# Residual tokens built by GpSimd in SBUF from the turned normed tokens, instead of being turned by TensorE and passed through DRAM

## The chip, the cores and the metric

The kernel runs on one core of one Trainium2 chip. The metric is device time in microseconds (us). The kernel before was timed three times: 315.67, 315.70 and 314.47 us, median 315.67 us. TensorE is PE in the profile, VectorE DVE, ScalarE ACT, GpSimd POOL, and SP is the engine that issues nearly all DMAs.

## The reference, cut to what matters

Input x is (4, 128, 32, 32): four images ("batches" here) of 128 channels and 1024 positions. Three layers follow each other, and each image passes them alone.

```
x = x + nin(softmax(q k^T) v)            # group norm, full attention over 1024 positions, one head
t = to_tokens(x)                         # (4, 1024, 128)
t = t + linear_attention(ln(t))          # softmax over keys, 4 heads
n = ln(t)                                # (t - mean) / sqrt(var + 1e-5), per token
logits = n @ router_w.T ; probs = softmax(logits) ; rw, re = top_k(probs, 2) ; rw = rw / rw.sum()
out = n
for e in range(8):
    out = out + combine[:, e:e+1] * (gelu(n @ w1[e] + b1[e]) @ w2[e] + b2[e])
t = t + out                              # so the result is t + n + the experts' sum
```

The change is about the term t + n of the last line, called the residual tokens. With spread s = sqrt(var + 1e-5) it is also n (1 + s) + mean.

## The kernel before, in words

Matrix products are made of fp32r parts: each operand is split into a high and a low part and three products are summed. An image's 1024 positions are 8 tiles of 128, or 2 halves of 512.

The program has two phases. In the first, each pass of a loop over images b runs the attention of image b, the linear attention's keys of image b-1 (la), and the end of the linear attention and the routing of image b-2 (lc). The first image has an opening of its own, the second a pass written out, and b = 2 and b = 3 are the passes of a hardware loop. In the second phase the experts of all four images run: 16 steps per image (2 halves by 8 experts), 64 steps in all, numbered through. The remaining linear attention and routing of images 2 and 3 are put between these steps, by tables that say at which step: TAIL_AT and END_AT (L67 and L68) for TensorE, ScalarE and VectorE, POOL_AT (L73) for the order on GpSimd. GpSimd doesn't step with the others: it takes its functions in that order, each held only by its own waits.

A step on the engines: TensorE makes the hidden product into one of two PSUM banks (L1468 to L1470), ScalarE applies Gelu (L871), VectorE multiplies by the token's share of the expert (L1354, both inputs in SBUF), ScalarE and VectorE split the product into high and low (L882, L1363), and TensorE makes the outward product five steps later. Some steps (WHOLE) use one product in full fp32 instead of three (L1831). Each engine runs its own program in order. PSUM banks are handed round: a unit (u0, lT, z0, ...) is a use of a bank, TensorE fills it after the earlier unit in the bank was drained.

What the change touches:

- second_norm (L595) makes the normed tokens w_n of t2 on GpSimd, token by partition, by layer_norm (L574): two small operations and a power (L581 to L585) for each half, then 8 of 128x128 (L590). TensorE turns w_n to channel by partition (turn_w), and its high and low parts stay in wT_hi and wT_lo.
- normed_residual (L598) adds w_n to t2 in 8 operations (L601). TensorE turns the sum in 8 transposes (turn_z, units z0 and z1), ScalarE drains them (L783) into out_s in the loop and xb later, SP stores 512 KB to DRAM (L400), and load_routed (L416) brings it back half by half into z_in (L422). result (L1366) adds it to the experts' sum in PSUM.
- first_norm (L604) makes the normed tokens u of the linear attention. In the second phase GpSimd has second_norm(2), first_norm(3), normed_residual(2), add_bout(3), second_norm(3), normed_residual(3), in this order. TensorE turns the halves of u at steps 15 and 17.
- The routing (route, L1176) is a chain of some 22 small VectorE operations from the turned logits (L1187) to the shares in comb (L1224). TensorE turns comb in two units c0 and c1, VectorE copies them (L1167), SP stores them (L407, L408). After the loop SP issues load_routed(0, 0) and load_routed(0, 1), and then the first shares (L463), broadcast to all partitions. The first multiply of the experts (L1354) waits for these. Image 3's first shares go the same way after step 42 (L441).
- b2_parts and cb_in: one product (L1827) adds the experts' output biases, weighted by the shares, with 16 rows of high and 16 of low parts.

## Time and profile before

| what | us |
|---|---|
| median of three runs | 315.67 |
| the profiled execution, its own time | 317.83 |
| its span, first to last instruction | 316.0 |
| PE busy | 301.5 (95%) |
| DVE busy | 256.2 (81%) |
| ACT busy | 200.4 (63%) |
| POOL busy | 156.9 (50%) |

The profile is of one execution. Its own time is 2.16 us above the median of the three. PE's busy time counts matmuls whose ends are modelled, so what counts below is the distance from one start to the next, and an idle gap that names who ended it. The first phase ends near 186 us.

### The profile page before, as it was taken

To read this page: it belongs to the slowest core of one execution; us is meant where nothing else is said; L and a number is where in the kernel's file an instruction comes from. 1 tells how busy PE (TensorE), PEld (TensorE's weight loads), DVE (VectorE), ACT (ScalarE), POOL (GpSimd) and SP (SyncE) were. 2 spreads that over 40 slices of the span, in tenths; PEclk is the share of its full clock that TensorE was granted. 3 is DMA by queue.
4 is the path that set the end of the run, shared out by engine and by line. 5 is a ranking of instruction groups with operands and counts; after the bars stand their busy time and mean duration, and the time that the engine had idled before them with its cause. 6 is when DMAs were issued, how large, how long until landed. Compare 5 with 4: busy or idle time off the path is not lost.

```text
span 316.0 us, 5527 instructions
## 1 busy us (share of the span) xinstructions
PE 301.5 (95%) x1592; PEld 239.3 (76%) x1592; DVE 256.2 (81%) x641; ACT 200.4 (63%) x352; POOL 156.9 (50%) x357
## 2 busy tenths in 40 slices
PE   7998989989999999999999998999999999998996
PEld 5787768866878887878888796887776876666885
DVE  5598698587587798987698986999998897796996
ACT  3468473656771587664279576559777556785992
POOL 3898890149941985970684400399932069100000
PEclk9599999999999999999999999999999999999999
DMA  5902000020000021000000118295602881227911
GB/s 129 337 14 66 2 0 2 0 68 0 1 3 0 2 66 44 26 12 0 0 1 0 66 25 242 115 419 221 208 8 97 311 317 40 73 81 299 350 34 66
DMA packets 12904, 29.61 MB, mean 94 GB/s; under 512 B 2208, under 2 KB 6224, under 8 KB 10960
## 3 DMA queue, kind: packets, MB, share of 16 engines
q1 hardware_dynamic: 12448, 28.87, 26.4%
q10 hardware_dynamic: 432, 0.46, 0.4%
q8 instruction: 10, 0.16, 0.2%
q14 instruction: 14, 0.11, 0.1%
HBM read 24.73 MB, written 4.59 MB: 93 GB/s over the span
## 4 chain that ended last, share of the span: by engine, by line
PE 71%; DVE 14%; DMA 6%; issue 4%; ACT 3%; SPq 1%; DVEq 0%; ACTq 0%
PE ring L1483 10%; PE ring L1468 8%; PE ring L1470 8%; PE ring L1469 8%; PE scores L1468 7%; PE scores L1470 7%; PE scores L1469 7%; PE ring L1831 3%; DMA k_both<-scratch_s 3%; DVE pT_lo L1071 3%; DVE prob L1064 2%; PE ring L1648 2%; PE ring L1626 2%; PE ring L1613 2%; DMA scratch_c<-xT 1%
## 5 line engine op out<-in xcount | busy, mean ns | idle before, releaser
L871 ACT ACTIVATE gel<-scores,b_c 128x512 f32<-128x512 f32 x64 | 43.8, 685 | 18.7 <-PE scores L1470 15.0
L1071 DVE TENSOR_TENSOR pT_lo<-ring,pT_hi 128x512 fp32r<-128x512 f32 x64 | 40.5, 681 | 9.7 <-ACT pT_hi L730 9.5
L724 ACT ACTIVATE prob<-prob,row_max 128x1024 f32<-128x1024 f32 x32 | 36.8, 1150 | 11.5 <-DVE prob L1064 11.5
L581 POOL TENSOR_SCALAR rstd<-lmv 128x4 f32<-128x4 f32 x16 | 4.5, 283 | 76.1 <-DVE lmv L1106 74.8
L1064 DVE TENSOR_SCALAR_CACHE_REDUCE prob<-scores 128x1024 f32<-128x1024 f32 x32 | 38.7, 1216 | 3.4 <-PE scores L1470 2.9
L730 ACT ACTIVATE pT_hi<-ring 128x512 fp32r<-128x512 f32 x64 | 34.6, 599 | 9.2 <-PE ring L1483 8.9
L1483 PE MATMUL ring<-ident,prob 128*128 128x128 f32 x256 | 33.9, 275 | 3.4 <-DVE pT_lo L1071 2.1
L1483 PEld LDWEIGHTS ring<-ident,prob 128*128 128x128 f32 x256 | 28.7, 140 | 8.4 <-DVE pT_lo L1071 2.7
L1468 PE MATMUL scores<-wT_hi,w_hi 128*128 128x512 f32 x64 | 30.1, 470 | 1.7 <-ACT gel L871 1.7
L1468 PE MATMUL scores<-k_both,q_hi 128*128 128x512 f32 x64 | 27.0, 422 | 0.7 <-DVE prob L1064 0.7
L1468 PE MATMUL ring<-pT_hi,v_hi 128*128 128x512 f32 x64 | 26.6, 416 | 0.8 <-DVE pT_lo L1071 0.8
L1470 PE MATMUL scores<-k_both,q_lo 128*128 128x512 f32 x64 | 25.1, 393 | 0.0
L1470 PE MATMUL scores<-wT_hi,w_lo 128*128 128x512 f32 x64 | 25.1, 392 | 0.0
L1469 PE MATMUL scores<-wT_lo,w_hi 128*128 128x512 f32 x64 | 25.1, 392 | 0.0
L1469 PE MATMUL scores<-k_both,q_hi 128*128 128x512 f32 x64 | 25.1, 391 | 0.0
L1470 PE MATMUL ring<-pT_hi,v_lo 128*128 128x512 f32 x64 | 25.0, 391 | 0.0
L1469 PE MATMUL ring<-pT_lo,v_hi 128*128 128x512 f32 x64 | 25.0, 390 | 0.0
L734 ACT ACTIVATE o_s<-ring 128x512 f32<-128x512 f32 x8 | 4.8, 598 | 27.4 <-PE ring L1470 27.4
L590 POOL TENSOR_SCALAR u<-t,rstd 128x128 f32<-128x128 f32 x32 | 20.4, 654 | 0.9 <-POOL rstd L585 0.9
L612 POOL TENSOR_TENSOR t<-t,bout_row 128x128 f32<-128x128 f32 x32 | 14.0, 476 | 12.6 <-PE ring L1483 7.5
L590 POOL TENSOR_SCALAR w_n<-t,rstd 128x128 f32<-128x128 f32 x32 | 17.2, 551 | 0.9 <-POOL rstd L585 0.9
L1468 PEld LDWEIGHTS scores<-wT_hi,w_hi 128*128 128x128 f32 x64 | 12.1, 189 | 6.7 <-ACT gel L871 4.1
(304 smaller groups left out, 794.5 us busy)
## 6 DMA issues: line engine op xcount, KB each, us to landing
pT_hi<-scratch_s SPq DMA_DIRECT2D x8, 1024.0 KB, 7.4
prob<-scratch_s SPq DMA_DIRECT2D x4, 1024.0 KB, 7.6
k_both<-scratch_s SPq DMA_DIRECT2D x3, 1024.0 KB, 5.9
z_in<-scratch_z SPq DMA_DIRECT2D x8, 256.0 KB, 3.2
out_dram<-out_s SPq DMA_DIRECT2D x7, 256.0 KB, 2.4
xb<-in_x_dram SPq DMA_DIRECT2D x3, 512.0 KB, 3.2
scratch_z<-out_s SPq DMA_DIRECT2D x2, 512.0 KB, 2.8
k_both<-scratch_s SPq DMA_DIRECT2D x4, 256.0 KB, 5.5
```

What stands on the lines that cost most here:

```text
L590: last = pool.tensor_scalar(dst[:, j, :], src[:, j, :], neg[:, j:j + 1], std[:, j:j + 1], ALU.add, ALU.mult)
L612: last = pool.tensor_tensor(tiles_piece(t2, n), tiles_piece(t1, n), tiles_piece(bout_b, n), ALU.add)
L724: act.activation(prob[:, i % 2, :], prob[:, i % 2, :], ACT.Exp, bias=row_max[:, i:i + 1], scale=-1.0, accum_out=row_sum[:, 0, i:i + 1]).th ...
L730: act.activation(tile_group(pT_hi, n, i), as_tiles(ps(place, unit)), ACT.Copy).then_inc(p_hi_made, 1)
L871: act.activation(half(gel, s % 2), scores[:, s % 2, :], ACT.Gelu, bias=b1_c[:, s % E:s % E + 1]).then_inc(e_gelu, 1)
L1064: dve.tensor_scalar(prob[:, i % 2, :], scores[:, 2 * (i % 2):2 * (i % 2) + 2, :].rearrange("p a t -> p (a t)"), -SCALE, None, ALU.mult, AL ...
L1071: dve.tensor_tensor(tile_group(pT_lo, n, i), as_tiles(ps(place, unit)), tile_group(pT_hi, n, i).bitcast(FP32), ALU.subtract).then_inc(drai ...
L1468: pe.matmul(dst, lh, rh, start=start, stop=False)
L1469: pe.matmul(dst, lh, rl, start=False, stop=False)
L1470: return pe.matmul(dst, ll, rh, start=False, stop=stop)
L1483: last = pe.transpose(dst[0:t.shape[-1], j * step:j * step + rows], t, ident[0:rows, 0:rows])
L1831: last = pe.matmul(dst, tile(w2_s, e), hs_ring[step % RING], start=e == 0, stop=e == closing(m, h))
```

## The change: what it does

- normed_residual, TensorE's turn_z, ScalarE's turn_z, the store (L400), the load (L422) and their semaphores go, for all four images.
- second_norm gets five small operations on 128x8 after its normed tokens, which put the spreads 1 + s and the high and low parts of the means into free columns of comb, and a wait at its end of the norm for the earlier store of comb's copy. They ride on the transpose c0 and on the store of the shares, which has 88 rows in place of 64.
- load_spreads broadcasts the 1 + s of each half to all partitions: 256 KB a half into SBUF. load_routed loads no residual, but two rows of means a half. These rows meet two rows of ones in b2_parts, so the product of the biases adds the means too.
- add_parts (8 operations of 128x128) adds wT_hi and wT_lo into z_of[m], and residual_of (8 more) multiplies by the spreads, both on GpSimd. Image 0's two and image 1's add_parts run before second_norm(2); image 1's residual_of after first_norm(3); image 2's after add_bout(3); image 3's after second_norm(3).
- The wait of add_bout for unit z1 goes. kT1 takes bank 0 in place of 2 in the loop. Image shares are staged in hw in place of z_in.

```diff
-ROUTING = dict(o=["o0", "o1"], w=["w0", "w1"], lg=["lg0", "lg1"], z=["z0", "z1"], c=["c0", "c1"])
+ROUTING = dict(o=["o0", "o1"], w=["w0", "w1"], lg=["lg0", "lg1"], c=["c0", "c1"])
...
-                  T3a=0, T3b=1, lg0=2, lg1=3, u0=0, u1=1, lT=2, z0=3, z1=0, kT0=1, kT1=2, PV0=3, T4a=0,
+                  T3a=0, T3b=1, lg0=2, lg1=3, u0=0, u1=1, lT=2, kT0=1, kT1=0, PV0=3, T4a=0,
...
-              + ROUTING["z"] + LINEAR["p"] + ROUTING["c"] + ["g"])
+              + LINEAR["p"] + ROUTING["c"] + ["g"])
...
-POOL_AT = dict(n2=2, n1=5, nr=12, ab=21, n2e=32, nre=38)
+POOL_AT = dict(n2=2, n1=5, z=12, ab=21, n2e=32, ze=44)
+SPREADS, MEANS = 2 * E, 2 * E + HALVES
+SHARE_ROWS = (2 * E + 3 * HALVES) * QUAD
+MEAN_ROW = 64
...
-    scratch_s = nc.dram_tensor("scratch_s", (B, HALVES * E * QUAD, P), FP32).ap()
+    scratch_s = nc.dram_tensor("scratch_s", (B, SHARE_ROWS, P), FP32).ap()
...
+        minus_one = sb("minus_one", [P, TILES])
+        means = sb("means", [P, TILES])
...
-        zT_early, cT_early = out_s[:, :], (z_in[0:TILES * E, 0:P], z_in[:, P:2 * P])
-        zT_late = xb[:, :]
-        cT_late = (xT[0:TILES * E, 0, :], xT[:, 1, :])
+        cT_early = (hw[0:SHARE_ROWS, 0:P], hw[:, P:2 * P])
+        cT_late = (xT[0:SHARE_ROWS, 0, :], xT[:, 1, :])
+        z_of = [z_in, xb, z_in, xb]
+        spread_of = [out_s[:, :]] + [m[:, :].bitcast(FP32) for m in (v_hi, v_lo, v_hi)]
...
-            def store_residual(place, lc, zT):
-                for unit in ROUTING["z"]:
-                    wait_drained(sp, place, unit)
-                    apart(sp)
-                sp.dma_start(scratch_z[bass.ds(lc * HALVES, HALVES)].rearrange("h c t -> c h t"),
-                             zT.rearrange("c (h t) -> c h t", h=HALVES)).then_inc(z_stored, 16)
...
-            def load_routed(m, h):
-                sp.wait_ge(z_stored, 16 * (m + 2))
-                apart(sp)
+            def shares_of(m, e0, ne):
+                rows = scratch_s[m, e0 * QUAD:(e0 + ne) * QUAD, :].rearrange("r t -> (r t)")
+                return rows.rearrange("(a t) -> a t", a=1).to_broadcast([P, ne * BANK])
+            def load_spreads(m):
                 sp.wait_ge(c_stored, 32 * (m + 2))
                 apart(sp)
-                sp.dma_start(half(z_in, h), scratch_z[m * HALVES + h]).then_inc(z_loaded[h], 16)
+                for h in range(HALVES):
+                    if m == B - 1:
+                        sp.wait_ge(z_ready[h], B - 2)
+                        apart(sp)
+                    sp.dma_start(half(spread_of[m], h), shares_of(m, SPREADS + h, 1)).then_inc(spread_loaded[h], 16)
+            def load_routed(m, h):
+                sp.wait_ge(c_stored, 32 * (m + 2))
+                apart(sp)
+                for n in range(2):
+                    row = MEANS + n * HALVES + h
+                    sp.dma_start(cb_in[MEAN_ROW + n:MEAN_ROW + n + 1, h, :].bitcast(FP32),
+                                 scratch_s[m, row * QUAD:(row + 1) * QUAD, :].rearrange("(a j) t -> a (j t)", a=1)
+                                 ).then_inc(c_loaded[h], 16)
                 parts = 2 * E * QUAD
                 for r in (0, QUAD * E):
...
-            sp.sem_inc(z_stored, 16)
             sp.sem_inc(c_stored, 32)
             load_x(1)
             load_x(2)
             with sp.Fori(2, B - 1) as b:
                 load_x(b + 1)
-                store_residual(loop_place(b), b - 2, zT_early)
                 store_shares(loop_place(b), b - 2, cT_early)
-            store_residual(loop_place(B - 1), B - 3, zT_early)
+            load_spreads(0)
             store_shares(loop_place(B - 1), B - 3, cT_early)
...
+            load_spreads(1)
...
-            sp.wait_ge(xb_read, B)
-            store_residual(TAIL, B - 2, zT_late)
             store_shares(TAIL, B - 2, cT_late)
+            load_spreads(2)
...
-            store_residual(END, B - 1, zT_late)
             store_shares(END, B - 1, cT_late)
             load_shares(3, 0)
+            load_spreads(3)
...
                 layer_norm(1, lc, t2, w_n, w_made)
-            def normed_residual(lc):
-                pool.wait_ge(w_made, lc * HALVES + HALVES)
-                for n in range(PIECES):
-                    last = pool.tensor_tensor(tiles_piece(t2, n), tiles_piece(t2, n), tiles_piece(w_n, n), ALU.add)
-                last.then_inc(z_made, 1)
+                pool.wait_ge(c_stored, lc * 32 + 32)
+                apart(pool)
+                at = 2 * E * QUAD
+                spread, high, low = (comb[:, 0, at + n * TILES:at + (n + 1) * TILES] for n in range(3))
+                std, neg = (rstd[1][:, i, :] for i in range(2))
+                pool.tensor_tensor(spread, std, minus_one[:, :], ALU.pow).then_inc(spread_chain, 1)
+                pool.tensor_scalar(means[:, :], neg, -1.0, 0.0, ALU.mult, ALU.add)
+                pool.tensor_scalar(high.bitcast(FP32R), neg, -1.0, 0.0, ALU.mult, ALU.add).then_inc(spread_chain, 1)
+                pool.wait_ge(spread_chain, lc * 2 + 2)
+                apart(pool)
+                pool.tensor_scalar(spread, spread, 1.0, 1.0, ALU.mult, ALU.add)
+                pool.tensor_tensor(low, means[:, :], high, ALU.subtract).then_inc(spread_made, 1)
+            def add_parts(place, m):
+                wait_drained(pool, place, "w1")
+                if m == 1:
+                    pool.wait_ge(xb_read, B)
+                for h in range(HALVES):
+                    if m > 1:
+                        wait_drained(pool, y_place(m - 2), f"y{h}")
+                    w_hi, w_lo = (half(w[:, m * T:(m + 1) * T], h).bitcast(FP32) for w in (wT_hi, wT_lo))
+                    dst = half(z_of[m], h)
+                    for n in range(QUAD):
+                        last = pool.tensor_tensor(tile(dst, n), tile(w_hi, n), tile(w_lo, n), ALU.add)
+                    last.then_inc(z_added, 1)
+            def residual_of(m):
+                for h in range(HALVES):
+                    pool.wait_ge(z_added, m * HALVES + h + 1)
+                    pool.wait_ge(spread_loaded[h], m * 16 + 16)
+                    dst, spread = half(z_of[m], h), half(spread_of[m], h)
+                    for n in range(QUAD):
+                        last = pool.tensor_tensor(tile(dst, n), tile(dst, n), tile(spread, n), ALU.mult)
+                    last.then_inc(z_ready[h], 1)
             def first_norm(lb):
                 layer_norm(0, lb, t1, u, u_made)
-            def add_bout(lb, routed):
-                if routed is not None:
-                    wait_filled(pool, routed, "z1")
+            def add_bout(lb):
...
-            pool.memset(b2_parts[:, :].bitcast(FP32), 0.0)
+            after(pool.memset(b2_parts[:, :].bitcast(FP32), 0.0))
+            after(pool.memset(b2_parts[MEAN_ROW:MEAN_ROW + 2, :].bitcast(FP32), 1.0))
...
-                    normed_residual(lc)
                 first_norm(la)
-                add_bout(la, place if lc is not None else None)
+                add_bout(la)
             batch(SECOND, 1, 0, None)
             pool.wait_ge(gn_made, 3)
             with pool.Fori(2, B) as b:
                 batch(loop_place(b), b, b - 1, b - 2)
             norms = gathered(
+                (0, lambda: add_parts(loop_place(2), 0)),
+                (0, lambda: residual_of(0)),
+                (0, lambda: add_parts(loop_place(B - 1), 1)),
                 (POOL_AT["n2"], lambda: second_norm(B - 2)),
                 (POOL_AT["n1"], lambda: first_norm(B - 1)),
-                (POOL_AT["nr"], lambda: normed_residual(B - 2)),
-                (POOL_AT["ab"], lambda: add_bout(B - 1, TAIL)),
+                (POOL_AT["z"], lambda: residual_of(1)),
+                (POOL_AT["ab"], lambda: add_bout(B - 1)),
+                (POOL_AT["ab"], lambda: add_parts(TAIL, 2)),
+                (POOL_AT["ab"], lambda: residual_of(2)),
                 (POOL_AT["n2e"], lambda: second_norm(B - 1)),
-                (POOL_AT["nre"], lambda: normed_residual(B - 1)),
+                (POOL_AT["ze"], lambda: add_parts(END, B - 1)),
+                (POOL_AT["ze"], lambda: residual_of(B - 1)),
...
-            def turn_z(place, lc, zT):
-                act.wait_ge(z_stored, lc * 16 + 16)
-                for n in range(HALVES):
-                    unit = f"z{n}"
-                    wait_filled(act, place, unit)
-                    act.activation(half(zT, n), ps(place, unit), ACT.Copy).then_inc(drained[place.bank(unit)], 1)
...
-                dve.wait_ge(z_loaded[h], m * 16 + 16)
+                dve.wait_ge(z_ready[h], m + 1)
                 if not first_batch(m):
                     dve.wait_ge(stored[h], m * 16)
-                dve.tensor_tensor(half(out_s, h), ps(place, f"y{h}"), half(z_in, h), ALU.add
+                dve.tensor_tensor(half(out_s, h), ps(place, f"y{h}"), half(z_of[m], h), ALU.add
...
-            def turn_z(place, lb):
-                pe.wait_ge(z_made, lb + 1)
-                for n in range(HALVES):
-                    turn(place, f"z{n}", tiles_of(t2, n))
             def turn_comb(place, lb):
                 pe.wait_ge(c_made, lb + 1)
+                pe.wait_ge(spread_made, lb + 1)
...
-                    pe.wait_ge(c_loaded[h], m * 32 + 32)
+                    pe.wait_ge(c_loaded[h], m * 64 + 64)
```

## Rows read from the trace of the kernel before

**Rows 1.** Busy time by stage: us, then each engine's busy us (instructions), clock, DMA share, GB/s.
```profile
91.50:141.70 50.20, 49.24 (x293) 39.93 (x293) 42.22 (x118) 30.53 (x58) 32.56 (x78) 1.00 0.07 24
141.70:191.00 49.30, 48.97 (x298) 40.73 (x299) 41.27 (x118) 30.22 (x58) 19.10 (x44) 1.00 0.07 21
215.00:240.00 25.00, 24.97 (x122) 18.87 (x122) 23.15 (x50) 20.50 (x36) 18.91 (x25) 1.00 0.36 126
265.00:292.00 27.00, 24.77 (x106) 17.13 (x104) 21.58 (x51) 19.29 (x32) 4.43 (x8) 1.00 0.35 130
```

**Rows 2.** The chain of waits in order of time: start, us, what.
```profile
185.99 1.79 DMA scratch_c<-z_in
...
190.79 4.67 DMA k_both<-scratch_s
...
234.28 0.87 PE scores L1483 x8
...
281.29 3.83 DMA scratch_c<-xT
285.26 4.75 DMA k_both<-scratch_s
```

**Rows 3.** VectorE's timeline, routing in pass b = 2: start, us, instruction.
```profile
122.43 0.29 DVE L1187 TENSOR_REDUCE logit<-ring 128x64 f32<-128x128 f32 x1 [0.21 <-PE ring L1671]
...
129.17 0.40 DVE L1203 TENSOR_TENSOR rt<-rt,falling 128x64 f32<-128x64 f32 x1
...
133.04 2.47 DVE L1071 TENSOR_TENSOR pT_lo<-ring,pT_hi 128x512 fp32r<-128x512 f32 x4
```

**Rows 4.** VectorE's timeline, the same instructions in pass b = 3.
```profile
172.57 0.29 DVE L1187 TENSOR_REDUCE logit<-ring 128x64 f32<-128x128 f32 x1 [0.21 <-PE ring L1671]
...
178.71 0.22 DVE L1203 TENSOR_TENSOR rt<-rt,falling 128x64 f32<-128x64 f32 x1
...
181.93 2.48 DVE L1071 TENSOR_TENSOR pT_lo<-ring,pT_hi 128x512 fp32r<-128x512 f32 x4
```

**Rows 5.** GpSimd's timeline in both passes.
```profile
127.32 3.52 POOL L556 TENSOR_SCALAR h_f<-xb,affine 128x128 f32<-128x128 f32 x8 [0.21 <-POOL affine L542]
...
173.65 3.36 POOL L612 TENSOR_TENSOR t<-t,bout_row 128x128 f32<-128x128 f32 x8 [3.77 <-PE ring L1483]
```

**Rows 6.** SP's timeline: the stores of the shares in both passes, the loads after them.
```profile
136.33 0.52 SPq L407 DMA_DIRECT2D scratch_s<-z_in  x1
...
185.49 0.45 SPq L407 DMA_DIRECT2D scratch_s<-z_in  x1
...
187.96 0.32 SPq L422 DMA_DIRECT2D z_in<-scratch_z  x1
```

**Rows 7.** GpSimd's timeline in the second phase.
```profile
201.78 0.43 POOL L581 TENSOR_SCALAR rstd<-lmv 128x4 f32<-128x4 f32 x1 [24.77 <-DVE lmv L1106]
...
211.55 0.19 POOL L581 TENSOR_SCALAR rstd<-lmv 128x4 f32<-128x4 f32 x1
...
215.93 10.02 POOL L590 TENSOR_SCALAR u<-t,rstd 128x128 f32<-128x128 f32 x8 [0.22 <-POOL rstd L585]
```

**Rows 8.** GpSimd's powers on gsum: us summary by form, ns min/median/max.
```profile
L537 POOL TENSOR_TENSOR gsum<-gsum,minus_half x3: 563/564/708, 7.5 to 57.3; 128x1 f32<-128x1 f32 x2, 128x2 f32<-128x2 f32 x1
```

**Rows 9.** TensorE's timeline: u turned at steps 15 and 17.
```profile
221.79 0.60 PE L1483 MATMUL ring<-ident,u 128*128 128x128 f32 x4
...
226.00 0.66 PE L1483 MATMUL scores<-ident,u 128*128 128x128 f32 x4
```

**Rows 10.** Around image 3's first shares: ScalarE's and TensorE's timelines.
```profile
279.07 0.58 ACT L783 ACTIVATE xb<-scores 128x512 f32<-128x512 f32 x1
...
292.12 0.50 PE L1468 MATMUL scores<-wT_hi,w_hi 128*128 128x512 f32 x1 [1.34 <-ACT gel L871]
```

**Rows 11.** VectorE's multiplies (L1354) by stretch: us, busy (count), clock, DMA.
```profile
224.00:230.00 6.00, 2.44 (x3) 1.00 0.60 210
...
292.00:311.00 19.00, 9.63 (x15) 1.00 0.52 178
```

29 lines of the change are left out of this document (11 added, 18 removed).

## The prediction

> **What bounds the kernel now.** I read the busy time by stage first. In the second phase TensorE is the bound: 24.97 us of the 25 from 215 to 240 are PE's, and DVE has only 1.85 us free there [rows 1]. In the two loop passes PE is busy 98 and 99%, DVE 84%. Then the chain of waits in order of time: it runs through PE except in three places that this change touches. After the loop it goes from the store of the shares to the first share load, 4.67 us to landing at 190.79, and around 281 to 290 it does the same for image 3, 3.83 us for the store and 4.75 us for the load [rows 2]. In pass b = 2 it goes through VectorE's routing, of which the timelines show more [rows 3, 4]. Last I read the timelines of POOL and PE for what POOL makes just in time [rows 7, 9].
>
> The reader should see that removed PE work is worth its time only where PE is what the chain goes through, and that POOL, although half idle, feeds PE at one point with no slack.
>
> **PE loses the turned residuals.** Eight transposes cost PE 0.87 us (234.28) [rows 2], so 3.5 us for four images.
>
> Pass b = 2 gives nothing of it. The routing starts from the turned logits, which PE makes before the residual, at 122.43, and ends when the pT_lo of tile 4 can start at 133.04, 10.61 us later [rows 3]. PE needs these drains before it goes on to the turned keys and comb. If PE comes 0.87 us earlier, it waits 0.87 us longer: 0.
>
> In pass b = 3 the same stretch took 9.36 us, 172.57 to 181.93 [rows 4], and there PE and DVE arrive nearly together. The difference of 1.25 us has a cause in the trace: in b = 2 POOL works beside the routing (group norm from 127.32 on), in b = 3 it ends at 173.65 + 3.36 = 177.0 and the operations after that are short (the multiply by falling 0.22 us against 0.40) [rows 3 to 5]. The change fills this hole. POOL does add_bout(2) up to 3.8 us earlier, as its wait for z1 goes, and then add_parts(0), residual_of(0) and add_parts(1): 24 operations at 3.36 / 8 = 0.42 us, 10.1 us [rows 5], or from about 173.3 to 183.4. So the routing of b = 3 becomes as slow as that of b = 2. The part behind 177.0 holds most of the difference; I take +0.85 us, bounds 0 and +1.25, and PE's 0.87 us are again not seen.
>
> Here the Trainium skill ("SBUF — State Buffer", Who interferes with whom) has a rule: a VectorE instruction with two SBUF inputs contends with a GpSimd instruction that reads SBUF, and one with a single SBUF input does not. By that rule the trace agrees: the pT_lo drains, with one input in PSUM, keep 0.62 us each in both passes, and the routing operations stretch. The rule also says that the loser waits for the whole instruction, which would make the cost in the expert phase much larger than the measured means give; that is a rival below.
>
> **The way to the first share.** SP issues the store of the shares 13.90 us after the turned logits in b = 2 (136.33 against 122.43) and 12.92 us after in b = 3 (185.49 against 172.57) [rows 3, 4, 6]. With a routing like that of b = 2, it comes +0.98 us later. Then SP issues load_routed for both halves: six DMAs from 187.96 until the first share load at 190.79, 0.47 us each [rows 2, 6]. The two residual loads go and four of means come: +2 issues, +0.9 us. The share load had 512 KB of residual in front of it; without them its 4.67 us should shrink. Between 0 and the 1.79 us of a small transfer as a floor (4.67 - 1.79 = 2.9), I take -0.6, nearer to 0, because the residuals were issued 1.4 to 2.8 us earlier and were partly through. Sum: +1.3 us, and it contains the +0.85, as PE waits at this gate for VectorE (the m3 copy stands behind the first multiply in VectorE's order). Bounds: -1.0 to +1.9. The spreads of image 0 are loaded and multiplied long before result(0, 0).
>
> **u comes later.** In the second phase POOL starts second_norm(2) when VectorE's statistics are there (201.78), and goes on to first_norm(3) at 211.55 with no pause; the 8 operations on u take from 215.93 to 225.95 [rows 7]. PE turns the second half at 226.00 [rows 9]: zero slack. It turns the first half at 221.79; half of 10.02 us after 215.93 is 220.9, about 0.9 us of slack. Into this chain the change puts five operations, before first_norm(3): a power on 8 columns, whose cost grows with the columns (564 ns for one, 708 for two [rows 8], so 144 a column and about 1.57 us for eight), four small ones at 0.2 to 0.3 us, and one semaphore round of 0.3 us: 2.9 us, bounds 2.3 (half the small ones hidden) and 4.0 (contended as the first ones at 201.78, 0.43 for 0.19). The first half then comes at 223.8, PE stands from 221.79, so 2.0 us. While PE stands, VectorE runs dry, POOL goes at 0.42 us an operation again, and the second half is there in time. Nothing behind absorbs it: PE has no idle time until 265. +2.0 us, bounds 0.5 and 3.3.
>
> **The rest of the second phase.** PE's transposes for image 2 go from the saturated stretch: -0.87 us. POOL does 40 operations on the residuals in place of 16, +24 x 0.42 = 10 us, beside VectorE's multiplies with two SBUF inputs. With POOL at work these take 2.44 / 3 = 0.81 us, without it 9.63 / 15 = 0.64 [rows 11], 0.17 us for each 2 us of POOL work: 0.9 us of VectorE time, of which most meets VectorE's idle time. +0.3 us, bounds 0 and 0.9. Both share loads of image 0 and 1 get 0.5 MB more in front; they are issued steps ahead: 0.
>
> **Image 3's shares.** The store took 3.83 us to land behind the 512 KB residual store, the same store 1.79 us in the loop [rows 2]: -2.0 us, and one issue less on SP, -0.5. ScalarE's two drains (0.58 us each, 279.07 [rows 10]) go from in front of a Gelu. PE can take of this only what it stood still, 1.34 us at 292.12 [rows 10], and with the transposes 0.87 us: at most 2.2, and up to 2.5 with smaller gaps (the stretch from 265 has 27.00 - 24.77 = 2.2 us of idle PE [rows 1]). Against it stands that add_parts(3) falls beside this routing, where POOL was idle before: it costs up to 0.85 us as in b = 3. I take -1.8 us, bounds -2.5 and -0.5.
>
> **The sum.** b = 2: 0. Loop end and first share: +1.3. u: +2.0. Image 2's transposes: -0.87. Contention: +0.3. Image 3: -1.8. Together +0.9 us. The profiled execution has a span of 316.0 and a time of 317.83, so 318.7 by it; against the median of the runs, 315.67, I forecast 316.6 us. The setup gets two more memsets and a wait on POOL, some tenths of a us in front of the group norm of image 1, where POOL waits for VectorE anyway: 0.
>
> **The rivals.**
> First, faster: u does not hold PE. POOL's pace on u is set by VectorE (1.25 us an operation, 10.02 / 8, against 0.44 in the loop, 3.52 / 8 [rows 5, 7]), and a later start meets a VectorE that has less to do. If the delay of u is under the 0.9 us of slack for the first half and the second catches up, and the share gate gains from the missing residual loads (0 in place of +1.3), the sum is -0.87 + 0.3 - 1.8 = -2.4: 313.3 us. For it speaks that every PE stall also unloads POOL; against it the zero slack at 226.00 and that the five operations are serial. It decides when the five cost less than 1 us net.
>
> Second, slower by a full block: each of POOL's 24 additional operations blocks VectorE for its 0.42 us. In the stretch 215 to 240 some 16 of them fall, 6.7 us, and VectorE has 1.85 us to give [rows 1], so it becomes the bound there by 4.9 us. That gives 316.6 + 4.6 = 321.2 us. For it speaks the rule of the Trainium skill named above; against it the means of 0.81 and 0.64 us.
>
> Third, slower by u alone: the five operations cost 4.0 us with contention, the share gate its upper bound 1.9 and image 3 gives only 0.9. Sum: 1.9 + 3.3 - 0.87 + 0.6 - 0.9 = +4.0, 319.7 us.
>
> Fourth, that it does what its words say and all four images give their 0.87 us, with image 3's gate: -3.5 - 1.3 = -4.8, 310.9 us. The routing in b = 2 speaks against it.
>
> **How the numbers follow.** Forecast 0.50, its own range 315.2 to 318.2. First rival 0.22, second 0.05, third 0.17, fourth 0.06. The range for 8 in 10 goes from 312.6 to 320.0; outside it are the fourth and the second rival and the outer ends of the first and third. About 0.5%, 1.6 us, is what a measurement of this kernel can tell from no change: below 314.1 is faster, above 317.2 slower. Of the forecast's 0.50, 0.32 fall within and 0.15 above, 0.03 below; of the first rival 0.18 below, 0.04 within; the fourth is below, the second and third above but for 0.04. So faster 0.27, same 0.40, slower 0.33.
>
> **What would show it.** In the profile after: the stretch from the turned logits to pT_lo in b = 3 near 10.2 us (right) or 9.4 (wrong). The first share landed about 10.3 us behind the issue of the store, before 9.97 (190.79 + 4.67 - 185.49), and the store itself 13.9 us behind the turned logits. An idle gap of PE of about 2 us before the turned u at step 15 whose releaser is POOL L590's line; without it the u step is wrong. The store of image 3's shares landing in about 1.8 us and no gap of PE over 0.5 us behind it. VectorE's L1354 at 0.8 us wherever POOL works; a mean over 1.0 us would be the second rival. The prediction is wrong as a whole if PE has no gap in the 20 us around step 15.

## The result, and the profile after

The changed kernel takes 324.37 us (median of 5 runs, 323.37 to 326.0), the kernel before 315.67 (314.47 to 318.25) in the same set of runs: a ratio of 1.028, 95% interval 1.0236 to 1.0324. Forecast were 316.6 us and a range from 312.6 to 320.0. The profiled execution of the changed kernel has a span of 322.7 us.

Busy time by stage, the stretches of [rows 1]:

```profile
91.50:141.70 50.20, 49.17 (x291) 39.76 (x289) 42.31 (x119) 30.28 (x57) 31.46 (x75) 1.00 0.08 24
141.70:191.00 49.30, 42.45 (x230) 34.53 (x229) 41.54 (x102) 23.70 (x45) 28.10 (x65) 0.93 0.00 0
215.00:240.00 25.00, 24.03 (x110) 17.88 (x110) 23.06 (x52) 18.45 (x31) 24.06 (x36) 1.00 0.61 242
265.00:292.00 27.00, 26.08 (x105) 17.19 (x104) 22.39 (x52) 19.85 (x31) 13.47 (x23) 1.00 0.25 88
```

Pass b = 2 is as before. In pass b = 3 PE is busy 42.45 us where it was busy 48.97, and its granted clock was 0.93. VectorE shows no loss there, 41.54 us busy against 41.27, with 102 instructions in place of 118. That is the trap of this profile: the time is lost on VectorE, and it is counted as busy. VectorE's timeline of the routing in pass b = 3 (start, us, instruction) has one line that stands out:

```profile
171.02 0.29 DVE L1223 TENSOR_REDUCE logit<-ring 128x64 f32<-128x128 f32 x1 [0.20 <-PE ring L1707]
171.35 0.22 DVE L1224 TENSOR_REDUCE rr<-logit 128x8 f32<-128x64 f32 x1
171.60 7.29 DVE L1225 TENSOR_TENSOR rt<-logit,rr 128x64 f32<-128x64 f32 x1
178.82 1.21 DVE L1100 TENSOR_SCALAR_CACHE_REDUCE prob<-scores 128x1024 f32<-128x1024 f32 x1
```

A subtraction of 128x64, with both operands in SBUF, takes 7.29 us. The same instruction takes 0.22 us in e8_one_input below. GpSimd's timeline beside it:

```profile
168.29 3.36 POOL L653 TENSOR_TENSOR t<-t,bout_row 128x128 f32<-128x128 f32 x8
171.60 3.37 POOL L635 TENSOR_TENSOR z_in<-wT_hi,wT_lo 128x128 f32<-128x128 f32 x8
174.93 3.39 POOL L645 TENSOR_TENSOR z_in<-z_in,out_s 128x128 f32<-128x128 f32 x8
178.27 3.49 POOL L635 TENSOR_TENSOR xb<-wT_hi,wT_lo 128x128 f32<-128x128 f32 x8
```

These are add_bout(2), add_parts(0), residual_of(0) and add_parts(1): 32 operations without a pause, all with two operands in SBUF. The first 25 kept their pace of 0.42 us; VectorE's operation was held from 171.60 to about 178.68, over 17 of them, and ran when the second operation of the last row began. I call this a hold: longer than one GpSimd instruction, and one-sided. What stood behind it, from ScalarE's and TensorE's timelines:

```profile
178.93 0.26 ACT L822 ACTIVATE rt<-rt 128x64 f32<-128x64 f32 x1 [6.75 <-DVE rt L1225]
183.49 0.69 ACT L802 ACTIVATE p<-ring,kst 128x512 f32<-128x512 f32 x1 [4.30 <-DVE kst L1162]
```

```profile
184.99 3.68 PE L1519 MATMUL ring<-ident,prob 128*128 128x128 f32 x16 [6.41 <-ACT p L802]
```

VectorE's key maxima come late, so ScalarE's softmax of the keys is late, so the PSUM bank is drained late, and PE stands 6.41 us. No wait names GpSimd here, since no semaphore of GpSimd was waited for. Behind the wait the granted clock was down too, 0.81 from 180 to 185 and then 0.50, which is 1.2 GHz:

```profile
185.00:190.00 5.00, 5.00 (x20) 4.71 (x21) 4.40 (x13) 3.78 (x7) 0.00 (x0) 0.50 0.00 0
```

So the hold itself is 7.1 us (7.29 less 0.22), and what this stretch lost beyond it goes to the slower clock and to other contention, which no run separates.

To follow where time is lost or won I use the starts of two series: the 32 exponentials of the attention's softmax on ScalarE (s0 to s31) and the 64 multiplies of the expert steps on VectorE (w0 to w63, L1354 before and L1390 after). The setup differs between executions of one kernel (s0 was 2.3 us earlier to 0.6 us later than in the profile of before, where it was at 17.9), so each row has its own shift at s0 taken off. Shifts against before, us; s20 to s21 lies in pass b = 2, s28 to s30 in pass b = 3. Of the four times of e10_wait_spaced the two highest, 320.52 and 322.32 us, are slow executions, so its medians stand in no comparison below.

| profile | s20 | s21 | s28 | s30 | w0 | w14 | w18 | w24 | w40 | w47 | w48 | w54 | w63 |
|---|---|---|---|---|---|---|---|---|---|---|---|---|---|
| after | 0.0 | -0.8 | -0.6 | 7.8 | 6.3 | 7.0 | 7.1 | 8.2 | 7.9 | 7.4 | 5.7 | 7.9 | 7.7 |
| e1_after_routing | 0.0 | -0.7 | -0.4 | -1.1 | -2.6 | -2.0 | 7.1 | 6.7 | 6.4 | 5.8 | 4.7 | 6.8 | 6.6 |
| e5_one_pause | 0.2 | -0.5 | -0.2 | 1.0 | -0.4 | 0.1 | 9.2 | 8.8 | 8.5 | 8.0 | 6.5 | 8.7 | 8.4 |
| e2_spaced | 0.1 | -0.6 | -0.3 | 0.6 | -0.8 | -0.1 | 0.0 | 1.2 | 0.9 | 0.3 | -1.6 | 0.5 | 0.3 |
| e3_stream_two (before, with a row added) | 0.0 | 0.0 | 0.0 | 1.1 | 0.4 | 0.4 | 0.4 | 0.4 | 0.3 | 0.3 | -1.7 | -1.7 | -1.3 |
| e6_all_spaced | 0.1 | -0.7 | -0.5 | 1.2 | -0.3 | 0.4 | 0.6 | 2.2 | 2.4 | 1.8 | 0.4 | 2.5 | 2.3 |
| e7_spaced_late | 0.0 | -0.4 | -0.3 | 0.9 | -0.5 | 0.2 | -0.7 | 1.8 | 2.0 | 1.4 | 0.3 | 2.4 | 2.2 |
| e8_one_input | 0.1 | -0.7 | -0.3 | -1.0 | -2.4 | -1.7 | -1.6 | -0.9 | -1.5 | -2.0 | -3.9 | -3.2 | -3.4 |
| e9_no_products | 0.1 | -0.6 | -0.3 | -1.0 | -2.5 | -1.8 | -1.6 | -1.1 | -1.7 | -2.2 | -3.2 | -3.2 | -3.2 |
| e10_wait_spaced | -0.1 | -0.8 | -0.4 | -1.1 | -2.6 | -2.0 | 2.7 | 4.0 | 4.2 | 3.6 | 2.2 | 4.3 | 4.1 |
| e11_wait_fours | 0.0 | -0.7 | -0.4 | -1.0 | -2.5 | -1.9 | 2.8 | 4.1 | 3.9 | 3.4 | 1.7 | 3.8 | 3.6 |
| e12_wait_spaced_late | 0.2 | -0.2 | -0.1 | -0.8 | -2.3 | -1.6 | -2.5 | -0.3 | -0.1 | -0.7 | -2.5 | -0.3 | -0.5 |
| e13_end_unscaled | 0.1 | -0.7 | -0.3 | -1.0 | -2.4 | -1.8 | 0.9 | 1.6 | 1.8 | 1.2 | 0.0 | 0.0 | 0.0 |

In the row of after the loss is in one step, s28 to s30, +8.4 us. The rest of the kernel comes out even: -0.7 in b = 2, -1.5 up to w0, +1.1 at w18 to w24, -1.6 at w48 and +2.1 right behind it.

One warning about the base of this table. It is one execution of before, 2.16 us above the median of its kernel. The row of e3_stream_two shows where some of that lies: this is the kernel before with GpSimd work added behind the loop, its residual still goes through DRAM, and from w47 to w48 it is 2.0 us faster than before all the same. So the gain of every row at w48 is not shown to be the change's.

### The profile page after: what moved, and what is told of

Read it like the earlier page. It is cut to its first block, busy times and chain, and to the rows that moved or that the text cites. A ratio compares the mean times of both kernels' runs of the same rounds, so it can differ in the third digit from the quotient of the medians.

```text
span 322.7 us, 5537 instructions
## 1 busy us (share of the span) xinstructions
PE 302.3 (94%) x1560; PEld 236.5 (73%) x1560; DVE 265.6 (82%) x641; ACT 197.5 (61%) x344; POOL 184.8 (57%) x411
## 3 DMA queue, kind: packets, MB, share of 16 engines
HBM read 24.77 MB, written 2.54 MB: 85 GB/s over the span
## 4 chain that ended last, share of the span: by engine, by line
PE 58%; DVE 19%; issue 10%; POOL 7%; ACT 4%; DVEq 0%; POOLq 0%; ACTq 0%
PE ring L1519 11%; PE scores L1504 6%; PE ring L1504 6%; PE scores L1506 6%; PE scores L1505 6%; PE ring L1506 5%; PE ring L1505 5%; DVE pT_lo L1107 3%; DVE prob L1100 2%; PE ring L1862 2%; POOL u L603 2%; PE ring L1662 2%; POOL w_n L603 1%; DVE pT_lo L1399 1%; ACT pT_hi L777 1%
## 5 line engine op out<-in xcount | busy, mean ns | idle before, releaser
L1519 PE MATMUL ring<-ident,prob 128*128 128x128 f32 x256 | 35.6, 285 | 9.6 <-ACT p L802 6.4
L1519 PEld LDWEIGHTS ring<-ident,prob 128*128 128x128 f32 x256 | 30.2, 146 | 14.9 <-ACT p L802 6.8
L1504 PE MATMUL scores<-k_both,q_hi 128*128 128x512 f32 x64 | 27.6, 431 | 0.8 <-DVE prob L1100 0.6
L1505 PE MATMUL scores<-k_both,q_hi 128*128 128x512 f32 x64 | 25.3, 395 | 0.0
L645 POOL TENSOR_TENSOR xb<-xb,v_hi 128x128 f32<-128x128 f32 x16 | 11.1, 725 | 16.7 <-DMA v_hi<-scratch_s 16.7
L603 POOL TENSOR_SCALAR u<-t,rstd 128x128 f32<-128x128 f32 x32 | 18.2, 587 | 0.9 <-POOL rstd L598 0.9
```

Source lines behind the costliest of these rows:

```text
L603: last = pool.tensor_scalar(dst[:, j, :], src[:, j, :], neg[:, j:j + 1], std[:, j:j + 1], ALU.add, ALU.mult)
L645: last = pool.tensor_tensor(tile(dst, n), tile(dst, n), tile(spread, n), ALU.mult)
L1504: pe.matmul(dst, lh, rh, start=start, stop=False)
L1505: pe.matmul(dst, lh, rl, start=False, stop=False)
L1519: last = pe.transpose(dst[0:t.shape[-1], j * step:j * step + rows], t, ident[0:rows, 0:rows])
```

## The experiments

The times of before in the three sets of runs were 316.69 (e1 to e5), 315.36 (e6 to e9) and 317.37 us (e10 to e13), medians of 19 to 23 runs. The ratios are against the before of the same set; differences of medians across sets are good to about 2 us.

**Moving the row: e1_after_routing and e5_one_pause.** The first waits, ahead of the sums of image 0, until the routing of the last pass is done; the second only until GpSimd's own add_bout(2) is through, a wait of one semaphore round.

```
 norms = gathered(
+    (0, lambda: pool.wait_ge(c_made, B - 2)),      # e1; in e5: pool.wait_ge(t1b_made, B - 1)
     (0, lambda: add_parts(loop_place(2), 0)),
```

> The changed kernel, but GpSimd waits for the shares of image 1 (c_made at 2, the end of the routing in pass b = 3) before add_parts(0), residual_of(0) and add_parts(1). In the changed kernel's profile one VectorE TENSOR_TENSOR with two SBUF inputs (128x64, in the routing) took 7.29 us beside GpSimd's unbroken row of TENSOR_TENSORs. Theory A, GpSimd's row locks that operation out: it takes 0.2 to 0.5 us again, PE's wait of 6.4 us in that pass goes, and the time falls by 7 to 8.5 us from 324.4, to 316 to 317. Theory B, the new bank of kT1 (0 in place of 2) makes PE wait for the key softmax whatever GpSimd does: the time stays within 1 us of 324.4.

> The changed kernel with one pause: GpSimd waits for its own last operation of add_bout(2) before add_parts(0), some 0.2 us, at the moment at which the held VectorE operation starts. If one break in the row is enough (the operation gets in at any gap and the next ones are each held for one GpSimd operation), the time is 316 to 318. If the row after the pause catches the same or the next operation again, one of them takes 3 to 7 us and the time stays between 320 and 325.

Measured: e1_after_routing 323.24 us (ratio 1.0218, 1.0137 to 1.0299), e5_one_pause 325.39 us (1.0305, 1.0237 to 1.0374). The totals hardly moved, nearly as Theory B had it, and yet both did what they should in pass b = 3: the hold there is gone (s30 at -1.1 and +1.0 in place of +7.8). That rules Theory B out, since kT1 has its new bank in both. But a hold came back elsewhere. VectorE's timeline of e1_after_routing in the expert steps, and GpSimd's:

```profile
224.96 8.14 DVE L1391 TENSOR_TENSOR hw<-gel,k_both 128x512 f32<-128x512 f32 x1 [2.76 <-ACT gel L910]
```

```profile
224.20 3.35 POOL L645 TENSOR_TENSOR xb<-xb,v_hi 128x128 f32<-128x128 f32 x8
227.52 3.35 POOL L653 TENSOR_TENSOR t<-t,bout_row 128x128 f32<-128x128 f32 x8
230.84 1.71 POOL L635 TENSOR_TENSOR z_in<-wT_hi,wT_lo 128x128 f32<-128x128 f32 x4
```

Multiply w16 stands 8.14 us beside residual_of(1), add_bout(3) and half of add_parts(2), 20 operations without a pause, and ends 0.55 us after the row does at 232.55. In e5_one_pause the same multiply takes 8.36 us. From w14 to w18 both kernels lose 9.1 us: the hold, and the clock behind it (0.50 from 225 to 230 in e1). In after this second row met VectorE too, and there they took turns (multiplies of 0.77 to 0.95 us). In e5 the first row still had 24 operations without a pause beside the routing, and no two-operand VectorE operation there took over 0.55 us. So the stall belongs to no place; whether a row catches an operation depends on how the two engines meet, and a small shift upstream decides it. Whoever had looked at the total alone would have called the first hold innocent.

**Breaking the row: e2_spaced.** A semaphore round between the operations of the first three functions only.

```
 last = pool.tensor_tensor(tile(dst, n), tile(w_hi, n), tile(w_lo, n), ALU.add)
+if spaced[0] and n < QUAD - 1:
+    after(last)                  # then_inc, and wait for it
```

> The changed kernel with a semaphore round between any two of the 24 GpSimd operations of add_parts(0), residual_of(0) and add_parts(1), at the same place beside the routing. Theory A (lock-out by an unbroken row): the gaps let VectorE in, no operation of the routing takes over 1 us, the time is 316 to 318. Rival A2 (any GpSimd work beside that operation holds it for as long as it lasts): the operation still takes 7 us or more and the time stays at 324 or above.

318.53 us (1.0051, 1.0012 to 1.009), just above the forecast of Theory A and 5.8 us less than after, with the same arithmetic and more semaphore rounds. GpSimd's rows become slower, eight operations in 4.3 us in place of 3.37, and no VectorE operation of the routing takes over 0.57 us. The loss goes with the hold. Whether it went because the row was broken or because everything behind it was moved a little, this run does not tell by itself: e5_one_pause moved the row by some 0.1 us, left 24 operations unbroken, and had no hold there either. e11_wait_fours below answers that for one multiply.

**A row in the kernel before: e3_stream_two.** 24 sums wT_hi + wT_lo into xb behind the loop. They started at 177 us, right behind add_bout(2), but the edit waits for a semaphore after every eighth sum. So 16 operations stood without a pause (from 173.72 to 180.42), then 8 and 8, and not the 32 of after:

```diff
+                for r in range(3):
+                    for n in range(TILES):
...
+                    last.then_inc(junk_made, 1)
+                    pool.wait_ge(junk_made, r + 1)
```

> The kernel before, with 24 more GpSimd TENSOR_TENSORs of 128x128 (sums of the high and low parts of image 0 into xb, not used) right after the loop, from about 177 us on, beside the second half of the routing of pass b = 3. Theory A: a VectorE operation with two SBUF inputs that meets the row is held for several us, up to 10, and the time rises by 3 to 10 us over before. Rival (contention only stretches each routing operation, as in pass b = 2): no operation over 1 us, the time rises by 0.5 to 1.5 us.

317.39 us (1.0044, 1.0002 to 1.0086). No hold: VectorE's routing operations were stretched to 0.55 us at most, s30 came 1.1 us late, w0 0.4. Theory A failed here, and the rival had both the size and the mechanism. The row was shorter than I had meant, so this run does not settle what 32 operations would have done to the kernel before. But with the 24 of e5_one_pause, and the 20 of the second row in after and e2_spaced, it shows that a row of 16 to 24 without a pause need not hold VectorE. Every long hold stood beside such a row; not every such row gave one.

**Spacing everything: e6_all_spaced, and e7_spaced_late,** where the five small operations of the spreads also stand behind the first norm.

> Every two-operand row that GpSimd runs behind the loop (the sums, the products and the sum with the output bias) is broken by a semaphore round between its operations; e2_spaced broke only the first three functions. Theory (a VectorE operation with two operands in SBUF can be held until an unbroken GpSimd row ends): no VectorE operation over 1.2 us, 317.5 to 318.7, as e2_spaced within 0.6%, since the second row happened to catch nothing there. Rival (it is the work of the 64 products and sums, however it is spread): longer rows cost more, 319.5 or above, with stretches all along the second phase.

> As e6_all_spaced, with the five small operations of the spreads behind the first norm (so u no longer waits for the power of eight columns, 3.5 us of GpSimd). Theory: the wait of PE for u at step 19 to 24 (1.1 us) goes, 316.5 to 317.6, 1.0 us below e6_all_spaced. Rival (the shares c then come later, or the step is hidden anyway): no difference from e6_all_spaced.

319.32 us (1.0079, 1.0042 to 1.0116) and 319.56 (1.0108, 1.0069 to 1.0147). No hold in either, and no gain over e2_spaced: its second row had not held anything. The 319.32 us lie above the range of the theory (317.5 to 318.7) and close to the rival's 319.5, and w63 is 2.0 us later than in e2_spaced: spacing rows that hold nothing has a cost of its own. Moving the small operations won 1.3 us up to w18 (-0.7 against +0.6) and lost 0.9 of it up to w24; that GpSimd's products then meet VectorE's multiplies earlier is a guess. My theory expected 1.0 us in the total; the rival was right.

**One operand in place of two: e8_one_input.** All sums and products become unbroken rows of as many scalings by 1.0; the residual loses its low part and its spread.

```
-last = pool.tensor_tensor(tile(dst, n), tile(w_hi, n), tile(w_lo, n), ALU.add)
+last = pool.tensor_scalar(tile(dst, n), tile(w_hi, n), 1.0, 0.0, ALU.mult, ALU.add)
-last = pool.tensor_tensor(tile(dst, n), tile(dst, n), tile(spread, n), ALU.mult)
+last = pool.tensor_scalar(tile(dst, n), tile(dst, n), 1.0, 0.0, ALU.mult, ALU.add)
```

> Sums and products replaced by unbroken rows of as many operations with one operand and the same tiles (a scaling by 1.0): the residual loses its low part and its spread. Theory (the lock-out belongs to rows with two operands in SBUF on both engines): none of the new rows holds VectorE, longest stretch under 1 us apart from the row of the output bias, 315 to 318. Rival (any unbroken GpSimd row does it): a stop of 3 us or more in pass b=3 again, 322 or above.

313.67 us (0.9934, 0.9894 to 0.9974), 10.7 us below after and below the forecast of 315 to 318. Here are the rows at the place of the first hold, GpSimd's and VectorE's:

```profile
167.52 3.36 POOL L653 TENSOR_TENSOR t<-t,bout_row 128x128 f32<-128x128 f32 x8
170.85 2.22 POOL L635 TENSOR_SCALAR z_in<-wT_hi 128x128 f32<-128x128 f32 x8
173.04 2.12 POOL L645 TENSOR_SCALAR z_in<-z_in 128x128 f32<-128x128 f32 x8
175.14 2.22 POOL L635 TENSOR_SCALAR xb<-wT_hi 128x128 f32<-128x128 f32 x8
```

```profile
170.83 0.22 DVE L1225 TENSOR_TENSOR rt<-logit,rr 128x64 f32<-128x64 f32 x1
```

The subtraction starts 0.02 us from the beginning of the new row, as in after, and is not held. The one-operand operations are also shorter, 8 in 2.2 us in place of 3.4, so the two kernels differ in the length of the row too; and one start that was not held is no proof, as e5_one_pause shows.

**No work at all: e9_no_products.** Every sum and product is left out, the waits, loads, counts and moves stay (the residual added is whatever xb holds).

> All sums and products of GpSimd are left out, with every wait, load and count of the change kept; the residual that is added at the end is whatever xb holds. It bounds what the removals, moves and loads of the change are worth without its GpSimd work. Theory: 312.5 to 315 (the end of the last image -1.5, b=2 -0.7, u +1.1, the rest nothing). Rival (the moves and loads cost themselves, through kT1 in bank 0 or the load of the shares behind the spread): 316.5 or above, and the products are then worth under 2 us in e6_all_spaced.

314.31 us (0.9931, 0.9895 to 0.9966), within the forecast. So the removals and moves are worth something: 3.2 us against the one profile of before (w63), 2.2 us by the ratio (1.1 to 3.3), 1.0 by the medians of the set. The lower figures are the safer ones: 1.0 of the 3.2 lies at w48, where e3_stream_two gained 2.0 without the change. Rows with one operand cost nothing on top (w63 at -3.4 in e8_one_input); the whole price of GpSimd's new work, 10.9 us at w63, came with the two-operand form. SP's timeline in e9_no_products, to be set beside [rows 6] and [rows 2]:

```profile
184.56 0.30 SPq L408 DMA_DIRECT2D scratch_s<-hw  x1
184.91 0.32 SPq L409 DMA_DIRECT2D scratch_c<-hw  x1
186.54 0.53 SPq L439 DMA_DIRECT2D cb_in<-scratch_s  x2
187.12 0.77 SPq L444 DMA_DIRECT2D cb_in<-scratch_c  x2
188.02 0.52 SPq L439 DMA_DIRECT2D cb_in<-scratch_s  x2
188.57 0.77 SPq L444 DMA_DIRECT2D cb_in<-scratch_c  x2
189.47 1.76 SPq L475 DMA_DIRECT2D k_both<-scratch_s  x4
```

The two loads of the means take 0.53 us of SP, against 0.32 for the one residual load that they replace, so all of load_routed takes 189.47 - 186.54 = 2.93 us, before 190.79 - 187.96 = 2.83. The first share load is issued 1.3 us earlier and took 3.9 us to land in place of 5.5 (medians of its four parts; 4.5 in e3_stream_two, with the residual loads still in front), and w0 then waits for a Gelu and no longer for the load.

**Waiting and breaking together: e10_wait_spaced, e11_wait_fours, e12_wait_spaced_late.** e1's wait, and from residual_of(1) on a semaphore round behind each operation (e10), or behind each fourth (e11); e12 is e10 with the five small operations behind the first norm.

> The first sums and products wait until the routing of the last pass is done (as e1_after_routing), and all rows from residual_of(1) on have a semaphore round between operations, so that the second row can't hold VectorE at weigh step 16 as it did there for 8.1 us. Theory: no VectorE operation over 1.2 us; e1_after_routing's 323.24 less 7.5 us of hold, 315 to 317.5, under e6_all_spaced since the routing has no GpSimd work beside it. Rival (the time of the products is paid wherever they stand): 318.5 to 320, as e6_all_spaced.

> As e10_wait_spaced, with a semaphore round only after every fourth operation. If a single round lets VectorE in, a hold lasts at most four operations (under 2.5 us, eight where add_bout's second half meets the sums) and the time is that of e10_wait_spaced within 1.5 us, 314.5 to 318. If a row of four holds as a row of twenty did, a VectorE operation takes over 3 us and the time is above 319.

> As e10_wait_spaced, with the five small operations of the spreads behind the first norm. Theory: u comes 3.5 us earlier on GpSimd and the 1 us at steps 19 to 24 goes, 0.5 to 1.2 us below e10_wait_spaced. Rival (as e7_spaced_late against e6_all_spaced: what u gains is lost to the products that then meet VectorE's two-operand work earlier): no difference.

Measured: e10 315.73, 319.79, 320.52 and 322.32 us (median 320.15, no interval), e11 320.67 (1.0108, 1.0044 to 1.0172), e12 318.13 (1.0039, 1.0012 to 1.0065). Neither of the first two is where I expected it, though no long hold is left in them; e11 came out above 319 with a longest operation of 1.39 us, so its second branch had the time and not the mechanism. e12 gained more than the forecast 0.5 to 1.2 us, 2.5 against e11, partly for a reason given below. e11_wait_fours shows the mechanism at its smallest, VectorE and then GpSimd at w16:

```profile
224.42 1.39 DVE L1400 TENSOR_TENSOR hw<-gel,k_both 128x512 f32<-128x512 f32 x1 [2.86 <-ACT gel L919]
225.74 0.94 DVE L1409 TENSOR_TENSOR pT_lo<-h_f,pT_lo 128x512 fp32r<-128x512 f32 x1
```

```profile
223.56 4.26 POOL L649 TENSOR_TENSOR xb<-xb,v_hi 128x128 f32<-128x128 f32 x8
```

The first four products of that row run to 225.27 (pace 0.42 us); the multiply, issued at 224.42, ends at 225.81, and 0.66 before that is 225.15. It waited for the third and the fourth product, although it could have come in between them, and got in at the semaphore round. The same multiply stood 8.14 us where nothing broke the row. So one semaphore round is enough to let VectorE in. It is one meeting in one profile, but with the five kernels in which every later row is broken by rounds (e6, e7, e10, e12 and e13, longest two-operand VectorE operation 0.98 us) it is what shows that the missing pauses carry the hold.

What cost e10 and e11 their gain is the step that my prediction had named, and the clock. TensorE's timeline of e10_wait_spaced, and its busy time by stretch (PEclk is the third number from the end):

```profile
220.55 0.66 PE L1533 MATMUL ring<-ident,u 128*128 128x128 f32 x4 [2.56 <-POOL u L603]
```

```profile
210.00:215.00 5.00, 5.00 (x22) 3.74 (x21) 5.00 (x9) 4.68 (x9) 3.99 (x9) 1.00 0.89 333
215.00:220.00 5.00, 2.99 (x14) 2.14 (x12) 4.59 (x8) 3.67 (x7) 4.78 (x5) 1.00 0.59 238
220.00:225.00 5.00, 4.45 (x19) 3.40 (x20) 2.11 (x5) 1.80 (x3) 4.69 (x10) 0.63 0.68 226
225.00:230.00 5.00, 5.00 (x19) 4.01 (x18) 3.31 (x9) 2.29 (x4) 4.37 (x9) 0.68 0.00 0
```

PE stands 2.56 us for the first half of u, and then it is granted 0.63 and 0.68 of its clock over ten microseconds, a mean of time at 2.4 and at 1.2 GHz. From w14 to w18 e10 loses 4.7 us.

How much of that is the wait, a kernel that does the same up to image 3 can say, e13_end_unscaled (below). In its profile:

```profile
223.29 0.66 PE L1536 MATMUL ring<-ident,u 128*128 128x128 f32 x4 [2.61 <-POOL u L603]
```

```profile
220.00:225.00 5.00, 2.39 (x13) 1.65 (x12) 2.91 (x5) 2.27 (x5) 5.00 (x9) 1.00 0.49 179
225.00:230.00 5.00, 5.00 (x30) 4.01 (x29) 4.40 (x11) 3.38 (x6) 4.45 (x8) 1.00 0.30 121
```

The same wait, PE no busier beside it (2.39 of 5 us against 2.99), and the granted clock stays at 1.00. It loses 2.7 us. So 2.7 is what the wait costs, and 2.0 more is what the fall to 1.2 GHz cost the execution in which it came. The same code had it in one profile and not in the other; what decides that, these runs do not show. e11's profile had the fall (0.77 and 0.55), e12's had neither the wait nor the fall. Between w14 and w18 the five small operations (3.7 us on GpSimd) are the only thing that e12 moves, and e12 gains 0.9 us there.

**The end: e13_end_unscaled.** e10_wait_spaced without the eight products of the last image.

> As e10_wait_spaced, without the eight products of the last image (its residual isn't multiplied by its spread). Theory (each of the eight stretches one VectorE operation of 0.66 us by 0.28): weigh steps 48 to 54 give back 2.1 us, the time is 2.0 to 2.4 us below e10_wait_spaced. Rival (PE is the bound there and hides it): under 0.7 us.

317.03 us (1.0011, 0.9966 to 1.0056). From w48 to w54 it loses 0.0 us where e10 and after lose 2.1. The profiles are 4.1 us apart at w63; 2.1 of that is at the end and 2.0 at w14 to w18, where both kernels do the same and only e10's clock fell, so only the 2.1 is the answer. VectorE's timeline of after there, and that of e13_end_unscaled at the same steps:

```profile
296.12 0.95 DVE L1390 TENSOR_TENSOR hs<-gel,k_both 128x512 f32<-128x512 f32 x1
297.00 0.95 DVE L1399 TENSOR_TENSOR h_lo<-hs,h_hi 128x512 fp32r<-128x512 f32 x1
...
303.08 0.68 DVE L1390 TENSOR_TENSOR hw<-gel,prob 128x512 f32<-128x512 f32 x1
```

```profile
291.92 0.68 DVE L1407 TENSOR_TENSOR hs<-gel,k_both 128x512 f32<-128x512 f32 x1
292.52 0.68 DVE L1416 TENSOR_TENSOR h_lo<-hs,h_hi 128x512 fp32r<-128x512 f32 x1
```

Eight VectorE operations at 0.95 in place of 0.68 us are the 2.1 us, 0.27 for each product: VectorE sets the pace there.

No version beat the kernel before and still computed the residual; e12_wait_spaced_late came nearest.

## Why the prediction was wrong, point by point

**The step that failed** is "the routing of b = 3 becomes as slow as that of b = 2. [...] I take +0.85 us, bounds 0 and +1.25". The work was placed rightly: 24 operations, forecast from about 173.3 to 183.4, stood from 171.60 to 181.76. Its price was not: that one stretch lost 8.4 us (s28 to s30), of which the hold is 7.1. Without the hold it lost 0.9 (e2_spaced, -0.3 to 0.6), which is my +0.85. The bounds came from the stretches that I had seen, operations beside rows of eight. I took a mean for the cost and did not ask what the length of the row does. The change removed the pauses of GpSimd (the wait for z1 among them) as well as adding work, and turned rows of 8 into one of 32. e11 shows that a pause ends a hold, and none outlasted the unbroken part of a row by more than the operation itself; whether an unbroken row starts one, the length alone does not decide.

**The rule that I weighed** was the one that mattered, and I used it too weakly. "SBUF — State Buffer", Who interferes with whom, in the Trainium skill, lets a VectorE instruction with two SBUF inputs contend with any GpSimd instruction that reads SBUF. For VectorE's side the trace agrees: drains with one operand in PSUM kept 0.66 to 0.69 us. On GpSimd's side the rows with two operands cost 10.9 us (after against e9_no_products at w63) and those with one, which are also shorter, -0.2 (e8 against e9); the rule makes no such difference, and these runs do not show whether the operands or the length of the row make it. That the loser waits for the whole instruction is too little for the holds, which lasted over some 17 to 20 instructions. At most places less than one whole instruction was lost: a 128x512 multiply grew by 0.27 us beside operations of 0.42. My second rival multiplied 0.42 us by 24 operations and gave 321.2; it missed by 3.2 us and had the wrong place, the stretch from 215 to 240, where after lost 1.1.

**The rest of b = 2 and b = 3.** "PE comes 0.87 us earlier, it waits 0.87 us longer: 0" failed by a small size. The stretch from the turned logits to pT_lo took 10.02 us in b = 2 (before 10.61 [rows 3]) and 8.67 in b = 3 of e9_no_products (before 9.36 [rows 4]). Each pass gave 0.6 to 0.7 us: the removed residual left the stretch itself, which I had taken as fixed by VectorE.

**The first share.** +0.9 us for two more issues was wrong: 0.1 measured. The -0.6 for the load looks too timid against the profile of before, -1.6 (5.5 to 3.9 us); against the 4.5 us of e3_stream_two, which has the old loads, it fits. Without the hold w0 comes 2.5 us earlier (e1, e8 and e9), where the forecast was +1.3, so this sum has the wrong sign.

**u.** +2.0 was the right mechanism at the right step, "PE stands from 221.79". In after PE stood 0.97 us for u's second half and lost 1.1 us from w18 to w24; e9_no_products has the same wait and loses 0.5, so some 0.6 of it is contention. Where the hold was taken away and VectorE kept GpSimd slow (e10 and e13), PE stood 2.56 and 2.61 us for the first half; that costs 2.7 us (e13), inside my bounds of 0.5 and 3.3, and 4.7 where the clock fell as well (e10), which I had no term for. The power of eight columns took 1.63 us (estimate 1.57), all five with their round 3.7 (estimate 2.9); the round itself, put at 0.3 us without a row, took 0.2.

**Image 3.** After is 1.6 us faster than before from w47 to w48, forecast 1.8, and the way there looks as forecast: store issued at 287.65, first load behind it at 289.34, so landed in under 1.7 us, and the PE gap of 1.34 us [rows 10] is gone. But the change is not shown to be the reason. e3_stream_two keeps the residual store in front, the load and ScalarE's two drains, and there SP's timeline and the busy time of the stretch of [rows 1] are

```profile
280.69 0.38 SPq L401 DMA_DIRECT2D scratch_z<-xb  x1
281.74 0.59 SPq L409 DMA_DIRECT2D scratch_c<-xT  x1
284.00 0.33 SPq L442 DMA_DIRECT2D k_both<-scratch_s  x1
```

```profile
265.00:292.00 27.00, 26.02 (x113) 18.45 (x112) 23.65 (x53) 21.39 (x35) 4.84 (x9) 1.00 0.40 144
```

The store landed in under 2.3 us behind the same 512 KB, PE was busy 26.02 us in place of 24.77, and w47 to w48 was 2.0 us faster. So neither the 3.83 us of [rows 2] nor the gap of [rows 10] is a fixed cost of the old route: they were there in the one execution of before that I had read and not in the other trace of that route. The term of -1.8 us rested on them, and no run shows any of it as the change's; that its number came out is luck. What I had not counted at all is that residual_of(3) falls on VectorE's busiest steps, and takes 2.1 us. "Contention +0.3" is this term, mis-sized: 2.1 at the end alone, and the 0.6 in w18 to w24.

Without the hold, the row of e2_spaced in the table gives the sum: -0.6 (b = 2), +0.3 (up to s28), +0.9 (routing of b = 3), -1.4 (first share), +0.8 (up to w18), +1.2 (u and contention), -0.9 (up to w47), -1.9 (w47 to w48, not shown to be the change's), +2.1 (its products) and -0.2, together +0.3. The forecast of +0.9 is near that by errors that cancel. By the medians of its set e2_spaced is 1.8 us above before, not 0.3; the profiled execution of before lies above its median. The hold of 7 to 8 us is what neither the forecast nor its range had.

**What stays open:** what decides whether a row holds VectorE or takes turns with it. The phase between the two starts does not: holds began 0.00, 0.12, 0.34 and 0.02 us into a GpSimd operation, and operations that began at 0.00, 0.13 and 0.34 in the 24 of e5_one_pause were not held. The totals of each kernel with a hold lie together, though (323.4 to 326.0 us for after, 322.0 to 325.2 for e1, 323.8 to 326.9 for e5), so it does not seem to come and go from one execution to the next; only one execution of each is traced. Three of the four held operations came right after a wait for a Gelu, the fourth (the first) in the midst of the routing, and others of both kinds passed. Nor do the runs show why the hold in after ended seven operations before the row did.

## What to carry to other kernels

Before work with two SBUF operands is put on GpSimd, look at what it makes of GpSimd's pauses: the number of such operations in a row that nothing interrupts can be a cost of its own, and a semaphore round between them bounds it, at a small cost where nothing was held. Look for a hold in the longest single VectorE instruction of each form, not in busy shares or waits, and move the row once before you believe that it is gone. When a stall is removed, the next one was often hidden by it: read the shift against before at fixed points, with each execution's setup taken off, and check against a second execution of before that a gain isn't one that the kernel has by itself.

## What the runs showed of the hardware

- A VectorE operation with two SBUF operands stood 7.29, 8.14 and 8.36 us beside unbroken GpSimd rows of two-operand operations, whose pace (0.42 us) did not change. Broken after four operations, the same multiply took 1.39 us; in the kernels that break every later row after each operation, the longest took 0.98. Rows of 16, 20 and 24 without a pause (e3, after and e2, e5) also passed with none over 0.95.
- VectorE operations with one operand in PSUM (pT_lo<-ring,pT_hi, 0.66 to 0.69 us) never stretched beside these rows, and GpSimd rows with one operand (8 in 2.2 us) cost nothing that w63 shows.
- It also works the other way: beside VectorE's two-operand multiplies single GpSimd operations on u (one operand, 0.44 us alone) took up to 1.92 us, in before as in e10 (1.99 in e12), and where these fall decides when u's first half is there (218.1 in e8, 220.5 in e10, from starts 0.4 us apart).
- PE waits of the same length did not always cost the same. In e10 a wait of 2.56 us, in a stretch in which PE was busy 2.99 of 5 us, stood before granted clocks of 0.63 and 0.68, and 4.7 us were lost; in e13, same code, a wait of 2.61 us and 2.39 of 5 us busy stood before a clock of 1.00, and 2.7 were lost. Behind the 6.41 us of after the clock was 0.50 from 185 to 190, and in e1 from 225 to 230.
- A store of 64 KB behind one of 512 KB took 3.8 us to land in one execution of the old route (before) and 2.1 in another (e3).
